# Layer 0's expert down product as one plain fp32 matmul per step instead of three fp32r passes

## The reference, cut to what matters

```python
        slots = jnp.einsum('bnd,bnes->besd', x, dispatch)
        gate = jax.nn.gelu(jnp.einsum('besd,edf->besf', slots, Wg) + bg[None, :, None, :], approximate=False)
        up = jnp.einsum('besd,edf->besf', slots, Wu) + bu[None, :, None, :]
        eout = jnp.einsum('besf,efo->beso', gate * up, Wd) + bd[None, :, None, :]
```

## Time and profile before

| | |
|---|---|
| time, median of 3 runs | 1195.64 us (1194.7 to 1196.39) |
| span of the profiled execution | 1191.2 us |
| PE busy | 999.9 us, 84% |
| DVE busy | 829.1 us, 70% |
| POOL busy | 647.9 us, 54% |
| ACT busy | 628.8 us, 53% |
| DMA, mean | 27 GB/s |
| layer 0's expert loop, first gate matmul to first combine matmul | 245.45 to 343.40 us |

### The profile page before, as it was taken

One profiled execution on the slowest core, in us unless ns is written; L12 is line 12 of the kernel. 1 busy time (PEld: TensorE's weight loads), 2 busy tenths in 40 slices (PEclk: granted clock), 3 DMA queues, 4 the chain that ended last, 5 costly groups with the idle time before them and its releaser, 6 DMA issues.

```text
span 1191.2 us, 18284 instructions
## 1 busy us (share of the span) xinstructions
PE 999.9 (84%) x4711; PEld 756.0 (63%) x4717; DVE 829.1 (70%) x1634; ACT 628.8 (53%) x1344; POOL 647.9 (54%) x676
## 2 busy tenths in 40 slices
PE   5799899988888695999999999999958587767364
PEld 3577566656676463888888888888846454445253
DVE  7676555579954679566666666666667799986886
ACT  2444566666632243666666666666632355543484
POOL 6011322256624333787878887887864478763400
PEclk9899999999999797999999999999987599978566
DMA  5000000022200000111111111111110000000001
GB/s 172 1 1 1 1 1 1 1 66 67 66 6 9 1 1 5 45 42 46 40 46 40 47 40 46 45 41 46 40 60 1 0 1 0 1 1 1 0 1 36
DMA packets 39779, 31.68 MB, mean 27 GB/s; under 512 B 4827, under 2 KB 36787, under 8 KB 39603
## 3 DMA queue, kind: packets, MB, share of 16 engines
q1 hardware_dynamic: 39731, 31.09, 9.0%
HBM read 30.02 MB, written 1.05 MB: 26 GB/s over the span
## 4 chain that ended last, share of the span: by engine, by line
PE 44%; DVE 23%; POOL 13%; issue 13%; ACT 5%; DMA 0%; POOLq 0%; SPq 0%; DVEq 0%; ACTq 0%; another core or an unknown queue 0%
PE psum L1809 37%; POOL hh L659 5%; POOL wgu L651 3%; DVE arena L1718 1%; DVE stats L1272 1%; PE psum L1927 1%; DVE xn L1285 1%; PE psum L1935 1%; PE psum L1875 1%; POOL rstd L599 1%; POOL hh L694 1%; POOL wdn L655 1%; DVE arena L1341 1%; PE psum L1824 1%; DVE arena L1714 1%
## 5 line engine op out<-in xcount | busy, mean ns | idle before, releaser
L1809 PE MATMUL psum<-xh,wgu 128*128 128x512 f32 x1408 | 374.0, 398 | 14.5 <-POOL wgu L685 9.9
L1809 PEld LDWEIGHTS psum<-xh,wgu 128*128 128x128 f32 x1408 | 268.9, 192 | 74.8 <-issue 15.3
L659 POOL TENSOR_TENSOR hh<-arena,hh 128x512 fp32r<-128x512 f32 x176 | 228.1, 1296 | 77.1 <-ACT hh L816 77.1
L1809 PE MATMUL psum<-hh,wdn 128*128 128x512 f32 x696 | 202.1, 399 | 27.8 <-DVE wdn L1451 14.9
L1601 DVE TENSOR_TENSOR arena<-psum,arena 128x512 f32<-128x512 f32 x176 | 121.6, 691 | 121.9 <-PE psum L1809 121.8
L1068 ACT ACTIVATE arena<-psum 128x512 f32<-128x512 f32 x176 | 105.3, 598 | 139.5 <-PE psum L1809 139.5
L1809 PEld LDWEIGHTS psum<-hh,wdn 128*128 128x128 f32 x696 | 127.3, 189 | 68.9 <-DVE wdn L1451 17.6
L816 ACT ACTIVATE hh<-arena 128x512 fp32r<-128x512 f32 x232 | 145.1, 625 | 26.0 <-DVE arena L1718 23.7
L1606 DVE TENSOR_TENSOR arena<-psum,arena 128x512 f32<-128x512 f32 x176 | 121.8, 692 | 32.4 <-DVE arena L1601 32.1
L1809 PE MATMUL psum<-arena 128*128 128x18 f32 (+7 forms) x810 | 133.9, 316 | 6.5 <-DVE X L1689 3.5
L816 ACT ACTIVATE arena<-psum 128x1024 f32<-128x1024 f32 (+8 forms) x106 | 72.3, 698 | 91.8 <-PE psum L1809 27.4
(11 more groups left out here) (291 smaller groups left out, 1808.9 us busy)
## 6 DMA issues: line engine op xcount, KB each, us to landing
w1gu<-in_w SPq DMA_DIRECT2D x88, 128.0 KB, 2.1
w1dn<-in_w SPq DMA_DIRECT2D x88, 64.0 KB, 1.9
egu<-in_egu SPq DMA_DIRECT2D x16, 256.0 KB, 2.6
edn<-in_edn SPq DMA_DIRECT2D x16, 128.0 KB, 2.0
arena<-in_w SPq DMA_DIRECT2D x1, 1536.0 KB, 5.9
X<-in_x SPq DMA_DIRECT2D x4, 256.0 KB, 3.8
out<-X SPq DMA_DIRECT2D x4, 256.0 KB, 2.3
arena<-in_ctxTd SPq DMA_DIRECT2D x1, 512.0 KB, 5.3
```

The costliest lines, as they stand in the source:

```text
L659: pool.tensor_tensor(hh[:, k, 1, :], h1[:, k, :], hh[:, k, 0, :].bitcast(F32), ALU.subtract).then_inc(hh_lo, 1)
L1809: return pe.matmul(dst, lhsT=lhsT, rhs=rhs, start=start, stop=stop)
```

## The change

`down0` becomes one plain fp32 matmul for each step, from the raw weights `edn` and from h0 itself. The halves of both are made no more: ACT's `hidden0_high`, POOL's `hidden0_low`, and DVE's `low0` and `down0_halves` are gone in all 32 steps. Three waits take new forms. `down0` waits for the transfer of the raw weights (`edn_in`) and for `h0_done`. `hidden0(n)` waits for `ed_ready` n-1, that is for the end of the down product of step n-2, the only reader of the tile that it writes over. `load_edn` waits for `ed_ready` in place of `wdn_lo`. In later layers only the offsets of the counts go.

```diff
             def load_edn(e, k, free):
-                sp.wait_ge(wdn_lo, free)
+                sp.wait_ge(ed_ready, free)
                 sp.dma_start(edn[:, k, :], ...).then_inc(edn_in[k], 16)
...
-            def hidden0_low(n, f):
-                pool.wait_ge(hh_hi, n + 1)
-                r = slice(0, LOW0)
-                pool.tensor_tensor(hh[:, f, 1, r], h0[:, f, r], hh[:, f, 0, r].bitcast(F32), ALU.subtract).then_inc(hh_lo, 1)
...
-            def hidden0_high(n, f):
-                act.wait_ge(h0_done, n + 1)
-                if later(n, 2):
-                    act.wait_ge(ed_ready, n - 1)
-                copy(hh[:, f, 0, :], h0[:, f, :]).then_inc(hh_hi, 1)
...
                 dve.wait_ge(eu_ready, n + 1)
                 dve.wait_ge(gelu_done, n + 1)
                 if later(n, 2):
-                    dve.wait_ge(hh_hi, n - 1)
-                    dve.wait_ge(hh_lo, n - 1)
-                    dve.wait_ge(hh_lo2, n - 1)
+                    dve.wait_ge(ed_ready, n - 1)
...
-            def down0_halves(n, k, f, loaded):
-                dve.wait_ge(edn_in[k], loaded)
-                if later(n, 2):
-                    dve.wait_ge(ed_ready, n - 1)
-                raw = edn[:, k, P * f:P * f + P]
-                dve.tensor_copy(wdn[:, f, 0, :], raw).then_inc(wdn_hi, 1)
-                dve.wait_ge(wdn_hi, n + 1)
-                dve.tensor_tensor(wdn[:, f, 1, :], raw, wdn[:, f, 0, :].bitcast(F32), ALU.subtract).then_inc(wdn_lo, 1)
-
-            def low0(n, f):
-                r = slice(LOW0, 512)
-                dve.wait_ge(hh_hi, n + 1)
-                dve.tensor_tensor(hh[:, f, 1, r], h0[:, f, r], hh[:, f, 0, r].bitcast(F32), ALU.subtract).then_inc(hh_lo2, 1)
...
-            def down0(n, k, f, evacuated=None):
-                pe.wait_ge(wdn_lo, n + 1)
-                pe.wait_ge(hh_lo, n + 1)
-                pe.wait_ge(hh_lo2, n + 1)
+            def down0(n, k, f, loaded, evacuated=None):
+                if f == 0:
+                    pe.wait_ge(edn_in[k], loaded)
+                pe.wait_ge(h0_done, n + 1)
                 if evacuated is not None:
                     pe.wait_ge(eo_sb, evacuated)
-                mm(bank(4 + k), wdn[:, f, 0, :], hh[:, f, 0, :], f == 0, False)
-                mm(bank(4 + k), wdn[:, f, 0, :], hh[:, f, 1, :], False, False)
-                mm(bank(4 + k), wdn[:, f, 1, :], hh[:, f, 0, :], False, f == 1).then_inc(ed_ready, 1)
+                mm(bank(4 + k), edn[:, k, P * f:P * f + P], h0[:, f, :], f == 0, f == 1).then_inc(ed_ready, 1)
```

More of the change, by code:

```diff
@@ L531, in load_dn @@
             def load_dn(c, k, free):
-                sp.wait_ge(wdn_lo, free + STEPS0)
+                sp.wait_ge(wdn_lo, free)
                 sp.dma_start(w1dn[:, k, :], A["w1"][bass.ds(c, 1), :, 2 * P:3 * P].rearrange("a p n -> (a p) n")).then_inc(w1dn_in[k], 16)
@@ L639, in expert_pair @@
                                 gate_up0_low(n + 1, k if f == 0 else 1 - k, 1 - f)
-                            if later(i, 1) or k or f:
-                                hidden0_low(n - 1, 1 - f)
                 expert_pair(0)
@@ L653, in down1_low @@
             def down1_low(c, slot):
-                pool.wait_ge(wdn_hi, c + 1 + STEPS0)
+                pool.wait_ge(wdn_hi, c + 1)
                 pool.tensor_tensor(wdn[:, slot, 1, :], w1dn[:, slot, :], wdn[:, slot, 0, :].bitcast(F32), ALU.subtract).then_inc(wdn_lo, 1)
             def hidden1_low(n, k):
-                pool.wait_ge(hh_hi, n + 1 + STEPS0)
+                pool.wait_ge(hh_hi, n + 1)
                 pool.tensor_tensor(hh[:, k, 1, :], h1[:, k, :], hh[:, k, 0, :].bitcast(F32), ALU.subtract).then_inc(hh_lo, 1)
@@ L965, in expert_pair @@
                         gelu(n, i * 2 + k, f)
-                        if later(i, 1) or k or f:
-                            hidden0_high(n - 1, 1 - f)
                         if f == 0 and later(i, 1):
@@ L1466, in expert_pair @@
                         hidden0(n, i * 2 + k, f)
-                        if later(i, 1) or k or f:
-                            low0(n - 1, 1 - f)
-                        if f:
-                            down0_halves(n - 1, k, 0, i * 16 + 16)
-                        elif k:
-                            down0_halves(n - 1, 0, 1, i * 16 + 16)
-                        elif later(i, 1):
-                            down0_halves(n - 1, 1, 1, i * 16)
                         if f and not last:
@@ L1603, in hidden1 @@
                 if later(n, 2):
-                    dve.wait_ge(hh_hi, n - 1 + STEPS0)
-                    dve.wait_ge(hh_lo, n - 1 + STEPS0)
+                    dve.wait_ge(hh_hi, n - 1)
+                    dve.wait_ge(hh_lo, n - 1)
                 dve.tensor_tensor(h1[:, k, :], bank(4 + k), u1[:, k, :], ALU.mult).then_inc(hid_done, 1)
@@ L2012, in expert_pair @@
                             starts = f == 0 and (later(i, 2) or (later(i, 1) and k == 1))
-                            down0(n - 2, 1 - k, f, i * 2 + (k - 2) if starts else None)
+                            down0(n - 2, 1 - k, f, i * 16 + 16 * k, i * 2 + (k - 2) if starts else None)
                 if later(i, 1):
@@ L2020, in _ @@
                 expert_pair(i)
-            down0(STEPS0 - 2, 1, 0, E0 - 2)
-            down0(STEPS0 - 1, 1, 1)
+            down0(STEPS0 - 2, 1, 0, 8 * E0, E0 - 2)
+            down0(STEPS0 - 1, 1, 1, 8 * E0)
             outputs_T(E0 // 2 - 1)
@@ L2162, in down1 @@
             def down1(n, k, slot, start=False, stop=False):
-                pe.wait_ge(hh_lo, n + 1 + STEPS0)
+                pe.wait_ge(hh_lo, n + 1)
                 mm(bank(6 + k), wdn[:, slot, 0, :], hh[:, k, 0, :], start, False)
@@ L2194, in chunk_pair1 @@
                         if k == 0:
-                            pe.wait_ge(wdn_lo, i * 2 + slot + STEPS0)
+                            pe.wait_ge(wdn_lo, i * 2 + slot)
                         if first and hf and slot:
@@ L2204, in _ @@
                         chunk_pair1(j * 3 + (NC1 // 2 * hf + 1 + r), hf)
-            pe.wait_ge(wdn_lo, 2 * NC1 + STEPS0)
+            pe.wait_ge(wdn_lo, 2 * NC1)
             for k in range(2):
@@ L2276, in down2 @@
             def down2(n, k, slot, hf, start=False, stop=False):
-                pe.wait_ge(hh_lo, n + 1 + STEPS0)
-                pe.wait_ge(hh_lo2, n + (1 - 4 * NC1) + STEPS0)
+                pe.wait_ge(hh_lo, n + 1)
+                pe.wait_ge(hh_lo2, n + (1 - 4 * NC1))
                 acc = bank(4 + 2 * hf + k % 2)
@@ L2328, in _ @@
             down2(4 * (NC1 + NC2) - 3, 1, 0, 1)
-            pe.wait_ge(wdn_lo, 2 * (NC1 + NC2) + STEPS0)
+            pe.wait_ge(wdn_lo, 2 * (NC1 + NC2))
             for k in (2, 3):
```

7 lines of the change are left out of this document (1 added, 6 removed).

## The result

| | before | after |
|---|---|---|
| time, median | 1196.02 us (1194.7 to 1197.5) | 1175.89 us (1175.23 to 1180.38) |
| ratio, with its 95% interval | | 0.9849 (0.9820 to 0.9878) |
| span of the profiled execution | 1191.2 us | 1174.2 us |
| expert loop, first gate matmul to first combine matmul | 97.95 us | 82.48 us |
| one pair of experts in mid-loop | 11.89 us | 9.86 us |

The changed kernel is faster by 1.5%. Four comparisons of the same program with different runs of before gave ratios of 0.9849, 0.9876, 0.9870 and 0.9867, so 1.3% is the better figure to keep. The forecast of 1180.1 us has the direction and nearly the size; the median of 1175.89 lies 1.1 us under the low end of its range, and so, by 0.1 and 0.4 us, do two of the three medians of the later comparisons (1179.10, 1176.94 and 1176.62).

What follows compares the result with a forecast made beforehand. DVE was taken to bound layer 0's expert loop, with PE next. PE's terms gave 16.1 us less, minus 0.6: 15.5 gained, so span 1175.7 plus 4.4 to the median, 1180.1 us; own range 1177.0 to 1183, wider range to 1188.0.

Steps and rivals of the forecast that it cites:

- low end: Bottom of the range, 1177.0 us: 2.6 us below the forecast, for 0.2256 us matmuls and a cheaper switch.
- What bounds the loop: Layer 0's expert loop: DVE sets the pace, with 12.0 us of work in a pair of 11.89 us; PE waits.
- What PE costs then: PE in the loop: gate and up 1.375 us, plain down product 0.857, transposes 0.87 a pair; a pair costs 9.8 us.
- The sum: Expert loop: PE's work ends 16.1 us earlier; less 0.6 us for first-pair waits and loop ends, 15.5 us gained.
- The moved waits: `hidden0(n)` waits for the down product of step n-2, `load_edn` for PE; both were to cost nothing.
- the ring: PE down(n-2), DVE h0(n), PE's up part of n+2: DVE needs 1.15 us, up to 1.9 more; cover 2.9 us.
- rival 2: Expert loop: h0's new wait makes a ring with PE, 38 us against 15.5 gained, 1218 us; chance 0.03.
- The tightest cover: Gate and up weight chain over ACT and POOL, a pair's first step: ready at 4.15 us, wanted at 4.49, slack 0.3.
- Rival 1: Expert loop: the gate and up weight chain binds, 4 us given back, 1184 us, or 1190; chance 0.15.
- Rival 3: After the loop: a later stage waits for something else, as weights, so the gain is lost, 1195 us; chance 0.02.
- rival 4: Down product in the loop: a plain call costs three records, not two, 13.7 us more, 1194 us; chance 0.03.
- rival 5: Expert loop: matmuls start closer, DVE paces a pair at 6.5 us, 43 us gained, 1153 us; chance 0.01.

Runs made afterwards that it cites:

- lower row of the table: Two kernels making no halves in the loop: three passes on halves written once, 9.13 us a pair (1175.8 us), and the changed kernel's plain product, 9.86.
- mixed kernel: Changed kernel with the down product of f = 1 in three fp32r passes on halves made again, f = 0 plain: 1190.46 us, 11.61 us a pair.
- run with the halves kept: Kernel before with the plain down product, all halves still made but unread: 1189.98 us, ratio 0.9968.

## Why the prediction was right, step by step

**What bounds the loop.** Right in the main. Making the halves set the pace and the matmuls didn't: 11.84 us a pair with the halves and the plain product, 9.13 without halves. That DVE is the engine behind it rests on its busy time, 11.45 of 11.84 us, and on the waits that lead back to it. One thing was missing in the reading: I took the durations of the earlier trace rows as DVE's own work. By the estimate above 3.0 of the 12.0 us were stretch beside POOL's work. For the sign it made no difference, since both left together; for the forecast of DVE's load it does: 6.5 us a pair were named, 5.65 were measured. A smaller misreading: the 6.5 us of idle time ahead of L1440 stand beside 31 instructions, which are not 31 waits.

**What PE costs then.** Each term held within 0.02 us a step. The 1.375 us for six matmuls and 0.87 us for the transposes gave a pair of 9.8 with the plain product; it is 9.86. The records are 590 to 596 ns where 593 were named, 64 in all. The price of the plain form over three passes was to be 0.17 us a step; the lower row of the table gives 0.73 / 4 = 0.18. Whether the switch between the two types costs a start-up was left open between two bounds: the step of 2.24 us against a sum of 2.23 leaves no room for one of 0.1 us.

**The sum.** The loop was to give 16.1 us less 0.6 for first and last waits, 15.5. It gave 15.47. Its parts: the first down product was to start 5.5 us after the first gate matmul and started at 5.8 (253.14 against 247.34), the last one was to end 79.1 us after it and ended at 79.8 (325.27 + 1.88), and the tail of 2.7 us stayed at

```profile
325.27 1.88 PE L1763 MATMUL psum<-arena,edn 128*128 128x512 f32 x4
328.51 1.06 PE L1952 MATMUL psum<-ident,arena 128*128 128x128 f32 x8 [1.36 <-ACT arena L806]
329.82 1.38 PE L1763 MATMUL psum<-arena 128*128 128x128 f32 x10 [0.25 <-ACT arena L806]
```

329.82 - 327.15 = 2.67 us. The 0.6 us set aside for waits of the first pair and for loop ends are nearly the 0.7 us by which the last product was late, and that is luck. No such wait is there: PE's only waits around the loop are the 2.7 us ahead of it and the 1.4 and 0.25 us of the tail, shown in the lines above. 0.25 us are a slip in my addition: 245.46 + 5.96 - 0.397 + 0.23 is 251.25 and not 251.0, so 5.79 us after the first matmul, and 5.80 were measured. The other 0.4 us are the 0.06 us by which a pair is longer than 9.80. So 15.47 against 15.5 flatters the sum; without the set-aside and with the slip mended it gives 15.9.

**The moved waits.** `hidden0` with its wait for the down product: right that the ring doesn't bind, since DVE now waits in it and PE doesn't. The mixed kernel shows at what point it does: once PE needs, within the step, something that is queued behind that wait. The price of 38 us for rival 2 was for every step; the mixed kernel paid at most 1.58 us a pair. `load_edn`: the transfers land within 2.0 us at the median and 4.2 at most, and no wait of PE names them, as forecast. 

**The tightest cover.** The chain of the gate and up weights had a slack worked out at 0.3 us. It didn't bind: the wait for POOL's `wgu` is 1.4 us in six pieces of at most 0.2, on PE's loads and not on its matmuls. Rival 1 is near but not reached. The run with the halves kept shows the same chain when POOL has its other work too: there PE waited 5.3 us for POOL's `wgu`.

**The rivals.** Rival 3 fell, since the end moved with the loop; rival 4, since 64 records stand there; rival 5, since PE is full at the old distances. For the last one the Trainium skill, on the page TensorE: Matmul & The Clock Gate, section Back-to-back issue gap, gives 131 ns for each matmul. No run here shows it; the rows stay at 226 ns. That DVE would then pace a pair at 6.5 us doesn't follow either. With 24 matmuls of 131 ns and the plain products and transposes as forecast PE needs 3.14 + 3.43 + 0.87 = 7.4 us, so the price of rival 5 holds only if the plain products were faster as well.

**What was mis-sized.** Two terms outside the loop. The first is the way from the profiled span to the median: I took the 4.4 us between 1191.2 and 1195.64 as fixed. In after it is 1.7 us (1175.89 - 1174.2). The execution that was profiled before was one of its faster ones: the medians beside the experiments were 1192.47 to 1193.54. That makes 2.7 us of the 4.2 us between 1180.1 and 1175.9. The other 1.5 us are the stages around the loop, -1.9 and +3.4 us. The size of these shifts could not be read from one trace of before, but that its span lay 3.5 us under the lowest of the three timed runs could. In the later executions time and span differ by 1.7 to 2.9 us. The low end was made of the matmuls' cost alone and had no room for either. It doesn't add up as given: 1180.1 - 2.6 is 1177.5 and not 1177.0, and the reasons named for it, 29 x 0.021 and 32 x 0.03 us, give 1.6.

## What to carry to other kernels

Sum each engine's work over one period of the loop and find the one that fills it. Compare each duration with the shortest of its kind, for part of the sum can be another engine's doing. If it isn't PE, a costlier form of the matmul that takes preparation off the other engine can be the faster one, up to the point where PE fills the period. Splitting the preparation over more engines was a poorer exchange here: by the waits, each half is a link in a chain and not only a load. Where an in-order queue gets a new wait, look at what stands behind it: moving work that is ready ahead of the wait, and with that away from POOL's, made the loop 10 us shorter here.

## What the runs showed of the hardware

- A plain fp32 matmul of 128 x 128 by 512 columns is two records 0.43 us apart, in the loop as in the earlier trace rows, and switching to and from fp32r costs nothing that shows (a step of 2.24 us against a sum of 2.23).
- DVE's operations on SBUF stretch beside POOL's: a product of 1024 columns 1.23 us without POOL's products and 2.18 and 3.51 with them; a cast of 128 columns a mean of 335 ns against 525, and a difference of 512 columns 692 against 991, without and with the halves of h0. Casts of 0.74 and 0.76 us ended within 0.1 us of POOL's instruction, and one of 0.21 us ran in a gap of POOL while ACT was busy. A busy share of DVE holds such time.
- Executions of one program differ by 1.3 us in the granted clock of the loop's first matmuls and by up to 3.4 us in one later stage. A change worth 2 us can't be read from a single pair of profiles here.
